# A two-lane decoder layer: 34 exchanges of neighbouring pieces in the table that interleaves the lanes

## The reference

```
x = ln(x + mamba(x))                 # in_proj, conv of 4 taps, selective scan of 256 channels x 16 states, out_proj
x = ln(x + cross0(ln_affine(x)))     # 16 heads of 64 over 32 context tokens, gated
x = ln(x + experts(x))               # shared ffn + top 2 of 8 experts, hidden 512
x = ln(x + window(x))                # 16 heads of 8, causal band of 128, rotary
x = ln(x + cross1(x))                # 16 heads of 8 over the context
x = ln(x + local(x))                 # depth 2: 8 heads of 64, blocks of 64 looking one back, rotary, then a gated gelu ffn of 341
```

## Time and profile before

| what | value |
|---|---|
| time, three runs | 1532.57, 1532.76, 1542.49 us (median 1532.76) |
| profiled execution | 1545.9 us, its span 1544.1 us |
| busy: TensorE, VectorE, ScalarE, GpSimd | 1269.2, 1046.3, 808.2, 395.7 us |
| mean granted TensorE clock | 0.911 |
| instructions | 23279 |

### The profile page before, as it was taken

How to read it: one execution, slowest core, us unless ns; L and a number is a source line. 1 busy time by engine, 2 the same in 40 slices (tenths; PEclk the granted TensorE clock), 3 DMA queues, 4 the chain that set the end, 5 groups by cost and what they waited for, 6 DMA issues and landing times. The chain is left out here.

```text
span 1544.1 us, 23279 instructions
## 1 busy us (share of the span) xinstructions
PE 1269.2 (82%) x8400; PEld 815.4 (53%) x8400; DVE 1046.3 (68%) x2162; ACT 808.2 (52%) x2180; POOL 395.7 (26%) x248
## 2 busy tenths in 40 slices
PE   5767878887998888789775888889689988988986
PEld 4412335884665556456531233579456654655663
DVE  4789976226887787378449998741378879746853
ACT  2466423453764556466627553336276636665663
POOL 0036633412000332032011665360400023202300
PEclk9789978997999989999987888989799999999997
DMA  8300001780000100001010000068400000000000
GB/s 298 123 0 1 0 1 54 254 268 19 2 1 1 35 21 15 1 15 28 2 28 0 1 0 1 1 201 263 130 1 2 1 1 22 22 1 14 22 8 14
DMA packets 42179, 72.21 MB, mean 47 GB/s; under 512 B 3793, under 2 KB 27473, under 8 KB 41810
## 3 DMA queue, kind: packets, MB, share of 16 engines
q1 hardware_dynamic: 28242, 56.30, 10.8%
q10 hardware_dynamic: 11776, 10.23, 2.6%
q0 software_dynamic: 2048, 4.20, 0.9%
HBM read 51.19 MB, written 13.24 MB: 42 GB/s over the span
## 5 line engine op out<-in xcount | busy, mean ns | idle before, releaser
L912 POOL TENSOR_TENSOR scratch<-scratch 128x1024 f32<-128x1024 f32 x64 | 149.7, 2353 | 140.4 <-DVE scratch L883 119.9
L634 POOL TENSOR_TENSOR small<-small,w_const 128x16 f32<-128x16 f32 x32 | 101.1, 3163 | 298.2 <-DVE small L1753 298.2
L731 PE MATMUL psum<-scratch,w_const 128*128 128x512 f32 x256 | 148.8, 713 | 18.5 <-POOL scratch L912 18.4
L883 DVE TENSOR_TENSOR_SCAN scratch<-psum,scratch 128x512 f32<-128x512 f32 x128 | 150.1, 1206 | 9.5 <-ACT psum L804 8.9
L634 POOL TENSOR_TENSOR rstd<-rstd,w_const 128x4 f32<-128x4 f32 x32 | 32.8, 1029 | 432.9 <-DVE rstd L596 430.3
L1706 ACT ACTIVATE scratch<-psum,mx 128x128 f32<-128x128 f32 x256 | 90.0, 376 | 72.7 <-DVE mx L1794 71.5
L804 ACT ACTIVATE psum<-scratch,a_neg 128x512 f32<-128x512 f32 x128 | 87.8, 690 | 61.2 <-DVE scratch L883 52.1
L1374 ACT ACTIVATE scratch<-psum,mx 128x256 f32<-128x256 f32 (+1 forms) x256 | 111.2, 465 | 10.0 <-DVE mx L1410 8.4
L720 PE MATMUL psum<-scratch,cb 96*128 96x512 bf16 x128 | 49.7, 428 | 60.6 <-DVE scratch L875 51.3
L1160 ACT ACTIVATE scratch<-psum,scratch 128x128 f32<-128x128 f32 x240 | 68.3, 368 | 54.7 <-PE psum L1101 54.6
L1541 PE MATMUL psum<-w_local,hT 128*128 128x512 f32 x192 | 91.2, 615 | 6.3 <-ACT hT L1523 5.1
(11 more groups left out here) (266 smaller groups left out, 3199.6 us busy)
## 6 DMA issues: line engine op xcount, KB each, us to landing
expert_weights<-in_expert_weights SPq DMA_DIRECT2D x61, 512.0 KB, 5.1
scratch<-scratch ACTq DMA_DIRECT2D x48, 128.0 KB, 2.3
folded_products<-expert_weights SPq DMA_DIRECT2D x8, 512.0 KB, 3.1
folded<-folded_products SPq DMA_DIRECT2D x8, 512.0 KB, 4.7
w_local<-in_local SPq DMA_DIRECT2D x1, 3122.0 KB
sorted_y<-scratch ACTq DMA_DIRECT2D x12, 256.0 KB, 5.6
scratch<-sorted_x SPq DMA_DIRECT2D x4, 704.0 KB, 6.7
scratch<-in_cross SPq DMA_DIRECT2D x1, 2624.5 KB, 12.9
```

Source lines behind the costliest of these rows:

```text
L634: t.eng.tensor_tensor(v, v, W("const", "neg_half").to_broadcast([P, v.shape[1]]), ALU.pow).then_inc(t.s[done], 1)
L731: ins = pe.matmul(sum_banks[c], ident, t.m.hC[:, 2 * ((n - 1) % 2) + c, :], start=(n == 1), stop=(n == NS))
L883: dve.tensor_tensor_scan(t.m.hs[:, n % 2, c, :], t.ps["dA"], t.m.dBu[n % 2][:, c, :], 0.0, ALU.mult, ALU.add)\
L912: t.eng.tensor_tensor(t.m.hC[:, 2 * (n % 2):2 * (n % 2) + 2, :], t.m.hs[:, n % 2], C, ALU.mult)\
```

## The change

Only the numbers of `TURNS` change, for TensorE, ScalarE and VectorE. All instructions, waits and buffers stay, and so does each lane's own order. A cut of the diff (the rest is further numbers of the same kind):

```diff
 TURNS = {
     "pe": [
-        5, 21, 4, 3, 1, 10, 2, 5, 4, 4, 2, 1, 6, 2, 3, 3, 3, 3, 3, 3, 5, 3, 3, 3, 3, 3, 3, 3, 3, 5, 3, 3, 3, 3,
+        5, 21, 4, 3, 1, 10, 2, 5, 4, 4, 2, 1, 6, 2, 3, 3, 3, 3, 3, 3, 5, 3, 3, 3, 3, 3, 3, 3, 2, 5, 4, 3, 3, 3,
...
     "act": [
...
-        6, 5, 5, 4, 2, 8, 4, 1, 8, 4, 1, 6, 3, 2, 4, 1, 5, 3, 1, 5, 3, 1, 6, 1, 1, 1, 1, 1, 1, 1, 1, 1, 1, 4, 4,
-        4, 1, 5, 3, 3, 6, 5, 5, 4, 2, 8, 4, 1, 8, 4, 1, 8, 4, 1, 8, 3, 1, 5, 3, 1, 6, 1, 1, 1, 1, 1, 1, 1, 1, 1,
-        1, 4, 4, 2, 1, 3, 1, 2, 3, 1, 2, 3, 1, 1, 3, 1, 2, 5, 1, 1, 1, 2, 1, 1, 2, 1, 1, 2, 2, 1, 1, 3, 2, 1, 1,
+        6, 5, 5, 4, 2, 8, 4, 1, 8, 3, 1, 7, 3, 2, 4, 1, 5, 3, 1, 5, 3, 1, 6, 1, 1, 1, 1, 1, 1, 1, 1, 1, 1, 4, 4,
+        7, 1, 2, 3, 3, 6, 5, 5, 4, 2, 8, 4, 1, 8, 4, 1, 8, 4, 1, 8, 3, 1, 5, 3, 1, 6, 1, 1, 1, 1, 1, 1, 1, 1, 1,
+        1, 4, 4, 2, 1, 3, 1, 2, 3, 1, 2, 3, 1, 1, 3, 1, 2, 4, 1, 2, 1, 2, 1, 1, 2, 1, 1, 2, 2, 1, 1, 3, 2, 1, 1,
...
```

## The result

The changed kernel takes 1551.88 us (median of 22 runs, 1541.91 to 1558.9). The kernel before, now also with 22 runs, takes 1542.45 us (1532.57 to 1559.7). The ratio is 1.0051 with a 95% interval of 1.0031 to 1.0071: slower by 7.9 us, 4.8 to 11. I had said 1536.0, slower by 3.45, range 1524 to 1546. The sign was right and the change is within 1%, but the time lies outside the range. Two things made the miss of 15.9 us: the level of the kernel before (1532.76 of three runs against 1542.45 of 22: 9.7 us), and the size of the change (9.4 us between the medians against 3.45: 6).

A forecast was written before the change was run, and what follows sets the result against it. No engine is full; the interleaving of two lanes on four in-order engines sets the time. Losses of 8.1 us less gains of 4.65 give +3.45, added to 1532.76 for 1536 us, range 1524 to 1546.

The forecast's parts named there:

- 116: TensorE, first scan stage: lane 0's broadcast goes from first to sixth and VectorE waits near 162 us; loss 0.9 us.
- VectorE 1120: Expert stage: lane 0's copy behind lane 1's delays ScalarE's DMA issue of 1079.03; loss 2.0 us, halved in the sum.
- TensorE 1058: Expert stage: lane 1's up product put ahead of lane 0's; loss 0.65 us, halved in the sum.
- TensorE 1577: Local stage, near 1470 us: a small loss, 0.45 us at most.
- VectorE 166: Near 200 us: lane 0's normalisation goes behind lane 1's scan and escapes GpSimd's hold; gain 2.3 us (0.7 to 2.75).
- TensorE 1458, 1594 and 1606: Transposes L1597 go before the other lane's L1549, so VectorE's copy begins sooner; gain 0.4 us each, 1.2 together.
- TensorE 1251: Lane 0's L1303 goes before lane 1's scores, for which ScalarE idled 2.56 us; up to 1.65 us, counted 0.8.
- The nothings: Remaining stretches, on TensorE and VectorE: no effect, as consumers come later; without cover at most 0.2 to 1.0 us each.
- TensorE 1639: Last stretch: lane 1's sum about 1 us earlier, but the end hangs on lane 0's; no effect.
- Cover: Rival: losses vanish in the other lane's work while gains stay, 1528.1 us, or 1526.8 with high gains; chance 0.35.
- The clock rival: Rival: the new order shifts TensorE's granted clock, moving matmul time 11 us, to 1547.5 or 1525 us; chance 0.15.
- "Nothing can be seen": Rival: losses and gains cancel, 1532.8 us; counted with the forecast and cover, without a chance of its own.

The follow-up runs named there:

- VectorE 1120 alone: Only the exchange of lane 0's and lane 1's L1243 copies on VectorE, against the kernel before: ratio 1.0028 (0.9997 to 1.0059).
- the gains only: Only the 9 stretches forecast as gains exchanged, against the kernel before: ratio 0.9966 (0.9932 to 1.0000), 5.3 us faster.
- the second measurement: The whole change once more, against runs of the kernel before on the same chip: ratio 1.0031 (0.9996 to 1.0066).
- Losses only: Only the 13 stretches forecast as losses exchanged, against the kernel before: ratio 1.0081 (1.0051 to 1.0111), 12.7 us slower.
- other losses: Only TensorE 1058, VectorE 1120, 1185, 1460 and ScalarE 697 exchanged, against the kernel before: ratio 1.0041 (1.0010 to 1.0073), 6.3 us slower.
- the change without the 13: The change with its 13 loss stretches back in the old order, against the kernel before: ratio 0.9936 (0.9901 to 0.9971), 10 us faster.
- the 21 with the clears: The change without its loss stretches, plus GpSimd's MEMSETs behind lane 1's scatter, against the kernel before: ratio 0.9959 (0.9930 to 0.9987), 6.3 us faster.
- The clears alone: Only lane 0's three GpSimd MEMSETs put behind lane 1's scatter issues, both expert stages, against the kernel before: ratio 0.9998 (0.9961 to 1.0034).

## Why the prediction was wrong, step by step

**The level: the step that failed most.** I made the sum against the profiled execution (1545.9 + 3.45 = 1549.4, which is 2.5 us from the measured median) and then carried it over to the median of three runs, 1532.76, as "an offset like that is not of the table". Two of those three lay at the very bottom of what this kernel does: 22 runs reach from 1532.57 to 1559.7, with the median 9.7 us higher. The sign that they did was in my own table, where one of three runs and the profiled one were 10 and 13 us above the other two. The range had no term for this at all. Put around 1542.45, the same range (8.8 below, 13.2 above) is 1533.7 to 1555.7 and holds 1551.9. The 15 us that I took as "about what a measurement of this kernel can tell from no change" was too coarse: 22 runs of each kernel tell the change to 3 us either way.

**The losses, term by term: right in place, 7% low.** 104, 116, 179, 541, 549, 647 all appear with the waits that I named and within 0.3 us. 116 and 179 are 0.3 larger: in 116 two broadcasts run together behind the group, to 163.72, and L878 waited for them. ScalarE 485 is 0.99, not 1.15. VectorE 1120 with TensorE 1058 is 1.70, not the halved 1.3. That these two are near is luck: the step up to 1085 us is the same to 0.02 us with VectorE 1120 alone, so this one came nearly whole (I had 2.0) and TensorE 1058 (I had 0.65) not at all. The halving was wrong up to 1085 us, and may be right at the stage's end (from 1073 to 1125 the traces with it need 1.5 to 5.2 us more than the first, those without it -0.8 to 3.9). TensorE 1577 is 0.62 at the full clock, not 0.45, and 1.69 with the slow stretch. VectorE 1460 and 1185 and ScalarE 697, for which I took 0.5, give 0.1 at most.

**The gains: 4.65 where the traces give 3.2.** VectorE 166 was forecast at 2.3 by the end of GpSimd's hold, and gives 1.77 against the first trace, 2.4 against the six traces that lose 0.63 there without it. What I hadn't seen is that the hold goes to the next normalisation; that cost nothing. TensorE 1458, 1594 and 1606 give 0.15 to 0.2, 0.6 and 0.2, not 0.4 each. TensorE 1251 gives 0.26: of the 2.56 us that ScalarE idled, with up to 1.65 to win, I had counted half of the 1.65, and a third of that came; what covered the rest isn't shown. This is the term most out of proportion.

**The nothings: right.** 0.9999, one step of 0.15. For TensorE 1639 the runs show no step of its own: all six traces that have it are 1.63 us shorter at the end, with matmuls 2.3 us shorter, but so is the trace of the gains only, where it isn't exchanged. The seven other traces set against the first aren't, so it isn't excluded that the exchange moves the clock there.

**The rivals.** Cover fell with the first steps: outside the expert stage every stall that I had sized over 0.3 us came through, in the local stages as well as where VectorE is full. The clock rival was half right: it moves this kernel's time, by far more than the table does (the slope within the runs of one kernel is 7 to 16 us per 0.01 of the mean clock), and slow stretches do follow the new stall at 1577 in four of the five traces that have it and in none of the others; but it doesn't answer each stall, and the changed kernel's mean clock was that of before in the shared runs. "Nothing can be seen" fell by the interval of 1.0031 to 1.0071.

**What is left over.** The stalls give +5.5 us, the ratio 7.9 (4.8 to 11), the second measurement 4.8 (-0.6 to 10.2). Between 5.5 and 7.9, 2.4 us are left; the slow stretch behind TensorE 1577 (1.69 less 0.62) is 1.1 of them. In the smaller kernels, what the stalls leave over mostly goes with the mean clock. Losses only, other losses and 1120 alone take 4.0, 4.5 and 2.7 us more than their stalls, at a clock lower than that of before by 0.0036, 0.0042 and 0.0026. Gains only, the change without the 13 and the 21 with the clears gain 2.1, 6.8 and 3.1 us more than theirs, at a clock higher by 0.0031, 0.0033 and 0.0026. The clears alone don't fit: 0.0030 higher, and no gain in the ratio. The others stay within 2.1 us of their stalls and 0.0017 of the clock. Whether the order moved the clock isn't shown: by the scatter within one kernel (some 0.005), a mean of 12 runs is sure to about 0.003.

## What to carry to other kernels

Where three runs and a profile of one kernel differ by 0.9%, as here, that scatter belongs into the range, and the level is the middle of all executions that are shown, the profiled one among them, not the median of three. That alone would have brought the level up to 1537.6 only, 4.8 us short of the later median. A swap of neighbours can be costed to some 0.3 us by asking whether the piece put first is ready and who idles for the piece put second; take the stall whole where engines are busy, since here a stall of over 0.3 us found no cover outside the expert stage. How the granted clock answers is a separate term, and here it was of the size of the sum itself. And a sum of small stalls is tested by the shift of each piece between traces and by groups of stretches on one chip, not by the total alone.

## What the runs showed of the hardware

A small VectorE instruction can stand still until GpSimd's clears are done: a 128x4 TENSOR_SCALAR of 0.16 us lasted 4.35 us, through three MEMSETs that follow each other, and ended with the last; a CAST of 0.17 us lasted 3.80 in the changed kernel. Which instruction is met differs between traces (L1181, L1191, L1219). Thirteen traces have the clears in place. In 15 of their 26 expert stages a small VectorE instruction takes over 2 us, and each time it ends 0.03 to 0.04 us after the last clear; in the four stages with the clears moved none does. The Trainium skill (GPSIMD Engine Reference, Specifications) speaks of contention; what these rows show is a full stop until a run of three GpSimd instructions ends.

The chips differ more than the kernels: before took 1542.5, 1572.2, 1564.3, 1543.9 and 1569.6 us as the median on the occasions that it ran. The largest steps between two traces of the same instructions lie in the expert stages (12.4 us at 255 to 300). The matmuls there are longer by 6.4 us together, so the clock has a part; what the weights' DMAs and the holds have isn't separated. TensorE's clock also moves a stage with few DMAs (a share of 0.02): 65 us of work became 73 at a mean of 0.84, in some executions and not in others.
